# Mamba block gated by a mixture of experts: the prologue reordered, and each final sum spread over three groups

## What is computed

```python
xn = (x - mean) / sqrt(var + 1e-5)
# attention part: a Mamba block
h = layernorm(xn) * norm_w + norm_b
x_ssm, z = split(h @ Win)                     # 256 + 256 channels
x_ssm = silu(conv1d(x_ssm, 4 taps, causal) + conv_b)
dt = softplus(x_ssm @ dt_w + dt_b)
B, C = x_ssm @ Bp, x_ssm @ Cp                 # 64 states
for t:  state = state * exp(dt * A) + (dt * x_ssm) * B;   y_t = sum over states of state * C
s = xn + ((y + x_ssm * D) * silu(z)) @ Wout
# expert part
shared = sum of 2 experts (128 -> 512 -> 128, gelu) on rmsnorm(xn)
scores = sigmoid(xn @ centroids)              # 8 experts, the best 2 of each token
routed = sum of the best 2, weighted by score / sum of scores
out = x + s * silu(xn + shared + routed)
```

## Time and profile before

| | us |
|---|---|
| median of three runs | 1833.13 |
| the profiled execution, its own time | 1835.35 |
| its span in the trace | 1833.4 |
| busy in the span: DVE | 1651.5 (90%) |
| PE, as matmuls | 1576.0 (86%) |
| POOL | 1439.9 (79%) |
| ACT | 1396.1 (76%) |
| mean granted clock of PE | 0.961 of full speed |

### The profile page before, as it was taken

How to read it: one execution, slowest core, us unless ns; L and a number is a source line. 1 busy time by engine, 2 the same in 40 slices (tenths; PEclk the granted TensorE clock), 3 DMA queues, 4 the chain that set the end, 5 groups by cost and what they waited for, 6 DMA issues and landing times. The chain is left out here.

```text
span 1833.4 us, 43669 instructions
## 1 busy us (share of the span) xinstructions
PE 1576.0 (86%) x13460; PEld 821.8 (45%) x13460; DVE 1651.5 (90%) x1785; ACT 1396.1 (76%) x2600; POOL 1439.9 (79%) x718
## 2 busy tenths in 40 slices
PE   1777648999999999999999999988989889898888
PEld 1543324444544444444444444444444444444444
...
GB/s 238 146 126 189 169 169 118 143 134 163 168 139 138 167 170 138 137 152 177 142 137 138 186 153 138 141 150 130 106 132 143 133 127 98 144 121 122 136 78 77
DMA packets 208967, 261.82 MB, mean 143 GB/s; under 512 B 26802, under 2 KB 104892, under 8 KB 208700
## 3 DMA queue, kind: packets, MB, share of 16 engines
...
q0 software_dynamic: 4096, 8.40, 1.5%
...
...
## 5 line engine op out<-in xcount | busy, mean ns | idle before, releaser
L704 POOL TENSOR_TENSOR arena<-arena 128x1024 f32<-128x1024 f32 x512 | 1201.3, 2361 | 217.2 <-DVE arena L1222 175.2
L1222 DVE TENSOR_TENSOR_SCAN arena<-arena,ps 128x512 f32<-128x512 f32 x944 | 1084.6, 1202 | 68.0 <-POOL arena L704 30.5
L944 ACT ACTIVATE arena<-arena,neg_A 128x512 f32<-128x512 f32 (+1 forms) x944 | 628.3, 713 | 65.7 <-DVE arena L1222 64.3
L1400 PE MATMUL ps<-arena 128*64 128x128 f32 x6912 | 470.9, 281 | 132.9 <-DVE arena L1222 105.8
L1414 PE MATMUL ps<-arena,ident 64*64 64x512 f32 x4096 | 559.2, 618 | 1.7 <-POOL arena L704 1.6
L1400 PEld LDWEIGHTS ps<-arena 128*64 128x64 f32 x6912 | 375.7, 138 | 357.9 <-DVE arena L1222 184.0
L1204 DVE TENSOR_TENSOR ps<-arena,ps 128x512 f32<-128x512 f32 x512 | 325.4, 681 | 35.6 <-PE ps L1386 31.7
L950 ACT ACTIVATE arena<-ident,b_turned 128x128 f32<-128x128 f32 x864 | 273.1, 388 | 0.0
L1414 PEld LDWEIGHTS ps<-arena,ident 64*64 64x64 f32 x4096 | 107.9, 132 | 164.0 <-issue 157.1
L671 POOL DMA_INDIRECT x_rms_by_expert<-arena,slots x64 | 70.0, 1093 | 132.9 <-DVE slots L1157 92.1
L887 ACT ACTIVATE arena<-ps,arena 128x256 f32<-128x256 f32 x160 | 67.0, 470 | 115.3 <-PE ps L1481 115.3
...
## 6 DMA issues: line engine op xcount, KB each, us to landing
arena<-c_scratch SPq DMA_DIRECT2D x128, 1024.0 KB, 8.6
...
arena<-w_shared_tiles SPq DMA_DIRECT2D x128, 64.0 KB
...
```

Of the source, the lines that this page charges most:

```text
L704: nc.gpsimd.tensor_tensor(products[:, i % RING, :, :], states[:, i % 2, :, :], c_rows[:, i // CG, i % CG, :].unsqueeze(1).broadcast_to((P, ...
L944: nc.scalar.activation(decay[:, 2 * i + h, :], dflat[:, ds(slot + h * L, L)], ACT.Exp, scale=aflat[:, ds(col, 1)]).then_inc(s["decay_ready ...
L1222: vector.tensor_tensor_scan(states[:, i % 2, h, :], decay[:, m, :], ps[bank][:], 0.0, ALU.mult, ALU.add).then_inc(s["scanned"], 1)
L1400: ins = mm(bank[HP * r:HP * r + HP, c * P:(c + 1) * P], u_turned[:, odd, c, h * P + HP * r:h * P + HP * r + HP], diag[:, c, :], start=True ...
```

## The change

The prologue is rebuilt, and the final sums are spread out.

- **Statistics.** BN_STATS, 32 instructions of a 128x128 tile, takes the place of reductions and squares; the variance that rms needs comes from the first LayerNorm's. xn is made in one pass for each tile, the rms rows by 32 scaled copies on ACT.
- **Order.** Scores, choice and slots come ahead of batch 0. Gates are turned by two transposes and stored in another layout.
- **Batches.** The turns are written out. x and z of a batch swap PSUM banks from turn to turn, and DVE convolves from PSUM (pad is gone). dt and u of batch p - 2 are finished in turn p, a turn later than before. ACT reads dt from PSUM four times (Relu and Abs, two halves), holds exp and ln in one table set, and makes the three bf16 parts of B. B transposed comes from four transposes of the copied rows, not from eight products.
- **Into the main part.** u of batch 0 is loaded and transposed inside the prologue. The first half of C is loaded ahead, and POOL drains no more: SP gives product_ready. The second half of C is loaded once u of batch 7 is stored. Block 0 has its rows turned at state 4, its tiles at 5 and 6, its output at 7 (before: 2; 3 and 4; 5 and 6).
- **Final sums.** In the group ahead, PE adds shared sum, xn and b2 (states 2, 4, 6), in the sum's group the routed rows (2, 4), in the group after x and the turned product (2, 4). ACT takes SiLU at its state 5 of the group after the sum's (with a table load of its own), POOL multiplies at state 7 of its own. The loads are issued two groups ahead, behind the second half of C.

SP, its loads and the stores of the prologue:

```diff
                 load_w2_shared(u, g)
-                if isinstance(u, int) and u + 1 in FINAL_OF:
-                    load_final(FINAL_OF[u + 1])
...
                     load_gates(NB - 1)
...
+                if isinstance(u, int) and u + 2 in FINAL_OF:
+                    load_final(FINAL_OF[u + 2])
...
+            for p in range(1, NB + 2):
...
+                    load_w2(0, e)
+                if p == NB - 1:
...
+                    sp.wait_ge(s["c_stored"], 16)
+                    sp.wait_ge(s["zeros_stored"], 16)
+                    for dst, src in ((dt_in, dt_d), (u_in, u_d)):
...
+                                     ).then_inc(s["dt_u_loaded"], 16)
+                if p < NB:
+                    store_x(p)
+                if p == NB - 1:
+
+                    sp.wait_ge(s["gates_stored"], 32)
+                    sp.wait_ge(s["z_stored"], 16 * NB)
+                    sp.sem_inc(s["product_ready"], 2 * CG)
+                    load_c(0, 0, 0, 0)
+                    load_b_row(0, 0, 0)
+                if 2 <= p:
+                    store_dt(p - 2)
+                if p == NB + 1:
+                    load_c(0, 0, 1, 0)
+                if 2 <= p:
+                    store_b(p - 2)
+                if p <= NB:
+                    store_c(p - 1)
+            sp.wait_ge(s["x_stored"], 16 * NB)
...
+            for n in range(IN_FLIGHT):
+                sp.wait_ge(s[f"x_sorted{n}"], 16 * TOPK * NT // IN_FLIGHT)
+            load_x_rows(0)
```

POOL:

```diff
-            for n in range(IN_FLIGHT):
-                pool.wait_ge(s[f"x_sorted{n}"], 16 * TOPK * NT // IN_FLIGHT)
-            pool.wait_ge(s["w1_scaled_stored"], 32)
-            pool.drain().then_inc(s["product_ready"], 2 * CG)
-
...
+                        if u in FINAL_OF and i == 7:
                             gate_attn(FINAL_OF[u])
```

ACT, the read of dt, the loop over the turns, and the final sums:

```diff
+            def take_dt(b):
+                nc.scalar.preload_act_table_set("natural_log_exp_and_others")
+                act.wait_ge(s["dt_projected"], b + 1)
+                if b >= 2:
+                    act.wait_ge(s["dt_u_made"], b - 1)
+                for h in range(NH):
+                    nc.scalar.activation(dt_raw[b % 2][:, h, :], ps[4 + h][:], ACT.Relu, bias=dt_b_cols[h])
+                for h in range(NH):
+                    ins = nc.scalar.activation(exp_abs[b % 2][:, h, :], ps[4 + h][:], ACT.Abs, bias=dt_b_cols[h])
+                ins.then_inc(s["dt_taken"], 1)
...
+            for p in range(NB + 2):
+                if 0 < p < NB:
+                    silu_z(p)
+                if p < NB:
+                    silu_x(p)
+                if p == NB - 1:
+                    for part in range(2):
+                        act.wait_ge(s["u_turned"], part + 1)
+                        nc.scalar.copy(utflat[:, part * L:(part + 1) * L], ps[part][:]).then_inc(s["ut_copied"], 1)
+                if 1 <= p <= NB:
+                    take_dt(p - 1)
+                    take_b_c(p - 1)
+                if p >= 2:
+                    third_part(p - 2)
...
+                if 1 <= p <= NB:
+                    second_part(p - 1)
+                    copy_bt(p - 1)
...
+                    if not block and i == 5 and u - 1 in FINAL_OF:
+                        silu_of(FINAL_OF[u - 1], block_ps[:])
+                    if not block and i == 6 and u - 2 in FINAL_OF:
                         copy_result(FINAL_OF[u - 2], block_ps)
                     if not block and i in (3, 5):
```

DVE, its convolution and the loop:

```diff
+                vector.tensor_scalar(diagD[:, h, :], ident[:], d_cols[h], None, ALU.mult).then_inc(s["diag_d_made"], 1)
+
+            def convolve(b):
+
                 for h in range(NH):
-                    dve.wait_ge(s["silu_x_made"], b * NH + (h + 1))
-                    ins = vector.tensor_scalar(conv_out[:, h, :], conv_in[:, h, 0:L], convw_sb[:, h, 0:1], None, ALU.mult)
+                    x_ps = ps[2 * (b % 2) + h]
+                    dve.wait_ge(s["x_projected"], b * NH + (h + 1))
+                    if b:
+                        dve.wait_ge(s["silu_x_made"], (b - 1) * NH + (h + 1))
+                    ins = vector.tensor_scalar(conv_out[:, h, :], x_ps[:], convw_sb[:, h, K - 1:K], None, ALU.mult)
                     for j in range(1, K):
-                        k += 1
-                        ins.then_inc(s["vector_step"], 1)
-                        dve.wait_ge(s["vector_step"], done + k)
-                        ins = vector.scalar_tensor_tensor(conv_out[:, h, :], conv_in[:, h, j:j + L], convw_sb[:, h, j:j + 1],
-                                                      conv_out[:, h, :], ALU.mult, ALU.add)
+                        link(ins)
+                        ins = vector.scalar_tensor_tensor(conv_out[:, h, j:L], x_ps[:, 0:L - j],
+                                                          convw_sb[:, h, K - 1 - j:K - j], conv_out[:, h, j:L],
+                                                          ALU.mult, ALU.add)
                     ins.then_inc(s["conv_made"], 1)
...
             choose_experts()
-            for b, odd in turns(dve):
-                convolve(b, b * NL + (base + NCONV - NL))
-                if isinstance(b, int) and b == 2:
-                    place_tokens()
-                parts_and_dt(b - 1, 1 - odd, b * NL + (base + 2 * NCONV - NL))
-            parts_and_dt(NB - 1, (NB - 1) % 2, base + NCONV + (NB - 1) * NL)
-
+            place_tokens()
+            for p in range(NB + 2):
+                if p < NB:
+                    convolve(p)
+                if p == 2:
+                    first_rest(0)
+                if p >= 2:
+                    dt_and_u(p - 2)
+                if 2 <= p <= NB:
+                    first_rest(p - 1)
```

PE, its turns, the first block and the final sums:

```diff
+            project_z(1)
+            for b in range(NB):
+                project_dt(b)
+                if b:
+                    turn_b(b - 1)
+                project_c_b(b)
+                if b + 2 < NB:
+                    project_x(b + 2)
+                    project_z(b + 2)
+                if b + 2 == NB:
+                    pe.wait_ge(s["dt_u_loaded"], 32)
+                    pe.wait_ge(s["silu_z_made"], NB)
+                    for part in range(2):
+                        for c in (2 * part, 2 * part + 1):
+                            for h in range(NH):
+                                ins = nc.tensor.transpose(ps[part][:, (c % 2) * DI + h * P:(c % 2) * DI + (h + 1) * P],
+                                                          u_in[:, 0, h, c * P:(c + 1) * P], ident[:])
+                        ins.then_inc(s["u_turned"], 1)
+            turn_b(NB - 1)
...
-            FIRST_X_AT, FIRST_TILES_AT, FIRST_OUT_AT, FIRST_NEXT_X_AT = 2, {3: (0, 1), 4: (2, 3)}, {5: (0,), 6: (1,)}, 7
+            FIRST_X_AT, FIRST_TILES_AT, FIRST_OUT_AT, FIRST_NEXT_X_AT = 4, {5: (0, 1), 6: (2, 3)}, {7: (0, 1)}, 7
...
-                            add_rows(FINAL_OF[u], 0, block_ps)
-                        if u in FINAL_OF and i == 2:
-                            add_rows(FINAL_OF[u], 1, block_ps)
-                        if u - 1 in FINAL_OF and i == 1:
+
+                        if u + 1 in FINAL_OF and i == 2:
+                            begin_final(FINAL_OF[u + 1])
+                        if u + 1 in FINAL_OF and i == 4:
+                            add_xn(block_ps, xn_final)
+                        if u + 1 in FINAL_OF and i == 6:
+                            add_b2(block_ps)
+                        if u in FINAL_OF and i in (2, 4):
+                            add_rows(FINAL_OF[u], i // 2 - 1, block_ps)
+                        if u - 1 in FINAL_OF and i == 2:
+                            open_result(FINAL_OF[u - 1], block_ps)
+                        if u - 1 in FINAL_OF and i == 4:
                             turn_back(FINAL_OF[u - 1], block_ps)
                         if u == NB * E - 1 and i == 2:
                             pe.wait_ge(s["last_gates_loaded"], 16)
                             pe.wait_ge(s["xn_loaded"], 16 * NB)
```

665 lines of the change are left out of this document (301 added, 364 removed).

## The result

The changed kernel takes 1770.66 us (median of 4 runs, 1767.62 to 1772.78), the kernel before 1833.02 beside it: a ratio of 0.966, interval 0.964 to 0.967. The forecast was 1770 (1747 to 1794).

| stretch | before | after | difference | forecast |
|---|---|---|---|---|
| start to first scan | 234.5 | 187.4 | -47.1 | -48 |
| group 0 | 47.1 | 43.9 | -3.2 | -5 |
| groups 1 to 39 | 936.6 | 936.6 | 0 | 0 |
| groups 40 to 63 | 601.6 | 589.5 | -12.1 | -10 |
| last scan to the end | 13.6 | 13.6 | 0 | 0 |

The account below looks back on a forecast made before the run. DVE was taken to bound the kernel, with two nearly equal chains (slots then scatters; eight batches) before the first scan. First scan -48, group 0 -5 and final sums -10 made -63: 1770 us, range 1747 to 1794.

Parts of the forecast that it names:

- Slots at 57: Prologue: statistics, scores at 42 and routing of 14.9 us would have the slots made at 57, before 116.8.
- ACT's and PE's loop matters more: Prologue batches: this loop, not DVE's 13.1 us of passes, sets a turn, taken as 13.9 us against 16 before.
- Scatters: Prologue, POOL: scatters take 117 us; run from 57, they end near 175 instead of about 234.5.
- Group 0, -5: First group of scans: 42 us, not 47; last state's stall on ACT's decays grows to about 11, other waits go.
- Final sums, -10: Groups 40 on: spreading the seven sums saves 22 us, late C rows cost 12, net -10.
- hidden in ACT's slack: Group after a sum: the extra 1.28 us table load for SiLU, in the middle of ACT's group, would cost nothing.
- The late C rows (+12): SP's queue delays the next group's first C half; DVE stops 2 us in each of six groups, +12.
- The serial turn of 17: Rival, prologue: turns stay at 17 us through PE at its lower level, BN_STATS at upper price: 1793; chance 0.2.
- slower: Rival, six groups with late C rows: each stops DVE over 12.5 us; at 15 us each 1848; chance 0.03.
- the scatters: Rival, prologue: scatters at 2.3 us apiece end at 212 and set the first scan, 26 later: 1796; chance 0.05.
- All as meant: Rival: C not late, a turn is DVE's 13.1 us, batch tail 4 shorter: 1750; chance 0.25.
- the forecast's own case: Whole kernel: the prediction's main case, a time of 1755 to 1787 us, chance 0.45.

Follow-up runs that it names:

- the run with three taps: Changed kernel with three convolution taps instead of four (oldest tap of each half left out, two DVE passes less a turn): 1763.18 us.
- the last combined run: Changed kernel with sums' loads moved back, batch 0's u transposed later, block 0's rows early, block a state earlier, first C half and B row a turn later: 1753.52 us.

## Why the prediction was right, and where not

- **Slots at 57, 59.45 measured.** BN_STATS of a tile took 0.20 us (3.19 for 16), between the lower end 0.14 and the 0.24 taken; the statistics and xn were ready at 26.0, not 28.1. Rms copies took 4.78 for 16 (5.0 taken). The choice began at 42.06 for a forecast 42, though its inputs were ready 2.1 earlier: PE's score products, which I had put beside ACT's work, stand in the chain when they are slow (with quick ones the choice began at 39.5). Missed, too: 2.5 us that DVE waits for the counting products, since PE has the transposes of h and batch 0's projections ahead of them.
- **Batches.** The first three turns took 35.0 us (35 forecast), and a turn then 13.5 (13.9). The step that failed is "ACT's and PE's loop matters more": PE did its dt products in 3.67 and 5.37 us in alternation (granted clock 1.00 and 0.68), ACT waited for it 1.25 us at most in a steady turn, and DVE's 13.1 with its issue bounded the turn, as the run with three taps shows. The number was near by luck: 13.9 and 13.1 are near, and so is ACT's own work, 12.4. From the end of batch 5's softplus to the first scan it was 26.6 us, 25 forecast (24 for the tail, 1 up to the scan), with DVE's 8.01 behind u's transposes in it, which I had taken for free. Slots 2.4 late, turns 3.1 early and the tail 1.6 late make 187.4 of 186.5.
- **Scatters.** They were to end near 175 and ended at 183.8: I had taken their pace for fixed, and it went from 1.74 to 1.95 us apiece. That cost nothing in this kernel; in the last combined run and with three taps DVE waited 5.2 and 7.6 us for POOL behind them.
- **Group 0, -5, -3.2 measured.** The stall of the last state grew to 12.98 (forecast 11), and the wait for the silu rows at state 3 came, but as 2.1 us of PE's and 3.3 of DVE's, not 5.
- **Final sums, -10, -12.1 measured, by other terms; that the totals agree is luck.** Term by term (the forecast's -9.5 was rounded to -10):

  | groups | forecast | measured |
  |---|---|---|
  | the sums' own, seven | -12.6 | -17.2 |
  | behind them, seven | -8.9 | -1.0 |
  | ahead of them, 45 to 60, six | +12 | +7.1 (5.4 of it at 48) |
  | 40 to 42 | 0 | -1.0 |

  The forecast for the groups behind had 4.7 for group 62, which keeps its stall. There PE waits 4.38 for a GELU of ACT, and ACT had not idled for 15 us, with the SiLU's load and the one back among its work: by this trace "hidden in ACT's slack" failed at that place, though no run takes the load away. The late C rows (+12) came to POOL, by 0.2 to 2.4 us, and not to DVE. In group 44, where I had worked it out: SP's wait ended at +16.1 us into the group, not +13.8, its five loads took 2.7 us to issue and not 5.9, and C left at +19.3 and landed at +27.6 (forecast 20.3 and 28.9); POOL, which was to want it at +26.3, came to it only 0.2 us before it landed. In place of six stalls of 2 us stood one of 5.4, of the weights in the same queue. I had looked at what is behind the wait, and priced the wrong row of it. It appears once because group 47 is the only one of the seven at which a batch ends too: the loads of batch 6's silu rows and batch 5's z stand ahead of the weights there. They cost little by their issue, since the weights left SP at +18.6 in group 47 and at +18.8 in group 44; but they landed 8.1 us after their issue in the one and 3.8 in the other.
- **The rivals.** The serial turn of 17 is out by 13.5, "slower" by C rows that never stopped DVE, the scatters by the first scan at 187.40, which doesn't wait for POOL. "All as meant" was right on what bounds the turn and on C, but the tail, group 48 and group 62 kept the time in the forecast's own case.
